# Expert picks by token group inside the feed-forward, bfloat16 slot tables for both choices at once, routing weights made in the routed stage

## The reference, cut to what matters

```python
xn = layernorm(x)                        # eps 1e-5
probs = softmax(xn @ router_w.T)         # 8 experts
val, idx = top_k(probs, 2)               # two experts for each token
w = val / (val.sum(-1) + 1e-8)
for e in range(8):                       # the reference computes all experts
    y[e] = new_gelu(xn @ w1[e].T + b1[e]) @ w2[e].T + b2[e]
out = x + sum over k of w[:, k] * y[idx[:, k]]
```

## Time and profile before

| what | value |
|---|---|
| median of 3 runs | 1114.38 us (1110.06 to 1118.21) |
| the profiled execution | 1115.24 us, span 1113.4 us |
| TensorE busy | 932.3 us (84%) |
| VectorE busy | 569.7 us (51%) |
| ScalarE busy | 574.5 us (52%) |
| GpSimd busy | 620.6 us (56%) |
| second_feed, first and last products near | 585 and 751 us |
| route_second | 751.6 to 781.7 us |
| routed, first transfers to the start of combine | 782.2 to near 1089 us |

### The profile page before, as it was taken

The page is one execution under the profiler, slowest core; times in us unless marked ns, Lnnn a source line. Parts: engine busy times, 40 slices in busy tenths (PEclk is TensorE's granted clock), DMA queues, the critical chain, the costliest instruction groups (busy, mean ns, idle before and its releaser), DMA issues. The chain is left out here.

```text
span 1113.4 us, 20955 instructions
## 1 busy us (share of the span) xinstructions
PE 932.3 (84%) x6700; PEld 843.5 (76%) x6700; DVE 569.7 (51%) x1280; ACT 574.5 (52%) x1201; POOL 620.6 (56%) x605
## 2 busy tenths in 40 slices
PE   6259699998699999969987999941699999999960
PEld 5248467776588988848886999941699999999960
DVE  1335489996555556338764465438233333333325
ACT  0021167776435656547645556630566666666640
POOL 0105658885625554435316998730477778778740
PEclk9669999998779999989997999965799999999985
DMA  7581234443011111100007000043466666666656
GB/s 250 163 296 51 65 134 149 164 147 138 1 58 58 58 58 58 58 1 1 2 1 310 1 15 24 20 180 151 143 189 195 206 194 201 193 191 200 200 154 244
DMA packets 64899, 137.04 MB, mean 123 GB/s; under 512 B 12505, under 2 KB 26578, under 8 KB 63490
## 3 DMA queue, kind: packets, MB, share of 16 engines
q1 hardware_dynamic: 55842, 113.34, 31.6%
q0 software_dynamic: 4848, 14.72, 3.8%
q10 hardware_dynamic: 4144, 8.16, 2.0%
HBM read 114.03 MB, written 24.39 MB: 124 GB/s over the span
## 5 line engine op out<-in xcount | busy, mean ns | idle before, releaser
L122 DVE CAST place<-place 128x512 fp32r<-128x512 f32 (+1 forms) x170 | 89.2, 567 | 166.8 <-PE moe_down L128 101.5
L2337 POOL TENSOR_TENSOR place<-place,place 128x512 fp32r<-128x512 f32 x84 | 138.1, 1644 | 51.5 <-DVE place L122 51.1
L2363 PE MATMUL moe_up<-place,place 128*128 128x128 f32 x1376 | 161.9, 276 | 0.0
L2363 PEld LDWEIGHTS moe_up<-place,place 128*128 128x128 f32 x1376 | 158.3, 193 | 0.0
L128 PE MATMUL moe_down<-place,place 128*128 128x256 f32 x1008 | 131.1, 286 | 0.4 <-POOL place L2337 0.4
L128 PEld LDWEIGHTS moe_down<-place,place 128*128 128x128 f32 x1008 | 123.4, 191 | 0.6 <-issue 0.6
L2422 ACT ACTIVATE place<-place 128x2048 f32 x44 | 84.0, 1912 | 43.6 <-PEq L2159 29.9
L2435 ACT ACTIVATE place<-moe_up,place 128x128 f32<-128x128 f32 x344 | 97.5, 366 | 13.5 <-POOL place L2337 13.2
L1425 POOL TENSOR_TENSOR place<-place,place 128x384 fp32r<-128x384 f32 x42 | 43.4, 1036 | 92.8 <-ACT place L1332 64.1
L787 PE MATMUL scores<-place,place 128*69 128x276 f32 x256 | 68.5, 412 | 11.1 <-DVE place L851 6.7
L1134 PE MATMUL ff_down<-place,place 128*128 128x256 f32 x486 | 70.7, 291 | 5.4 <-POOL place L1425 4.9
(11 more groups left out here) (273 smaller groups left out, 1987.2 us busy)
## 6 DMA issues: line engine op xcount, KB each, us to landing
place<-w_remainder SPq DMA_DIRECT2D x172, 256.0 KB, 3.8
place<-in_w_dram SPq DMA_DIRECT2D x4, 4096.0 KB, 13.3
place<-gate_rows SPq DMA_DIRECT2D x24, 384.0 KB, 4.8
place<-in_w_dram SPq DMA_DIRECT2D x16, 512.0 KB, 3.7
w_remainder<-place SPq DMA_DIRECT2D x16, 512.0 KB, 3.0
place<-value_rows SPq DMA_DIRECT2D x64, 64.0 KB, 2.3
place<-choices ACTq DMA_DIRECT2D x5, 768.0 KB, 8.4
place<-in_patches_dram SPq DMA_DIRECT2D x9, 384.0 KB, 4.1
```

The costliest lines, as they stand in the source:

```text
L122: return eng.tensor_copy(out, x)
L2337: pool.tensor_tensor(lo[f], raw[f], hi[f].bitcast(F32), ALU.subtract).then_inc(h_split, 1)
L2363: last = pe.matmul(p1[u][k // HK][:, (k % HK) * P:(k % HK + 1) * P], ws[u][:, c, k * P:(k + 1) * P], xT[u][:, c, :], start=(c == 0), stop= ...
```

## The change

Three things change.

1. **second_feed** gets a function pick(g) on VectorE: for the three tiles of group g it picks both experts from the logits themselves (the softmax keeps their order), into two one-hot tiles self.hot of bfloat16, and keeps the highest and second highest logit in self.best. It is called for group g - 2 at the end of round g, and for the last two groups at the end. The new tiles lie where head_mask and stats were.
2. **route_second** no longer has the softmax and the choice. hits is the sum of the two one-hot tiles. The small steps of the two choices are made at once on 36 columns. ids, places, blocks and tile numbers are copied to bfloat16, so that the wide comparisons and products read bfloat16 on both inputs. One of the two row tables of each choice is scaled on ScalarE. The owners are computed after the tables.
3. **routed**: the weights (sum of exponentials, reciprocals, products) are made on VectorE ahead of its first split, and TensorE makes rise(0) ahead of turn_x(1).

The diff, cut to its core:

```diff
@@ second_feed, vector
+                def pick(g):
+                    rank = self.rank.unsqueeze(1).to_broadcast([P, G, E])
+                    dve.wait_ge(lg_read, g + 1)
+                    for k, src in enumerate((of(self.lg, g), sc)):
+                        best = self.best[k][:, G * g:G * g + G]
+                        link(dve.tensor_reduce(best, src, AX_X, ALU.max))
+                        link(dve.tensor_tensor(tmp, src, inner(best, E), ALU.is_equal))
+                        link(dve.tensor_tensor(tmp, tmp, rank, ALU.mult))
+                        link(dve.tensor_reduce(top, tmp, AX_X, ALU.max))
+                        link(dve.tensor_tensor(of(self.hot[k], g), inner(top, E), rank, ALU.is_equal))
+                        if k == 0:
+                            link(dve.scalar_tensor_tensor(out=sc, in0=of(self.hot[0], g), scalar=-BIG, in1=src, op0=ALU.mult, op1=ALU.add))
...
                         moments_of(3, x, g + 2)
+                    if g >= 2:
+                        pick(g - 2)
                 add_down(NG - 1)
                 moments_down(NG - 1)
                 add_h(NG - 1)
+                pick(NG - 2)
+                pick(NG - 1)
@@ route_second, scalar
-                act.wait_ge(step, 2)
+                act.activation(spare, self.ident[:, 0:8], ACT.Exp)
+                act.wait_ge(shifted, 2)
                 act.activation(lg, lg, ACT.Exp).then_inc(exped, 1)
+                act.activation(self.best[1], self.best[1], ACT.Exp).then_inc(exped, 1)
+                for k in range(2):
+                    act.wait_ge(matched, k + 1)
+                    act.activation(rows[k][:, :, 0, :], match[:, k], ACT.Copy, scale=consts["row"][:, k:k + 1]).then_inc(scaled, 1)
@@ route_second, vector
-                link(dve.tensor_reduce(total, lg, AX_X, ALU.max))
-                link(dve.tensor_tensor(lg, lg, inner(total, E), ALU.subtract))
+                link(dve.tensor_tensor(hits, self.hot[0], self.hot[1], ALU.add))
                 link(dve.tensor_copy(tri, consts["tri"]))
                 link(dve.memset(ones, 1.0))
...
-                self.choose(lg, first, second, self.weight, tmp, dve, link)
...
+                dve.tensor_tensor(hits[:, NT - 1, :], hits[:, NT - 1, :], consts["valid"][:, NT - 1:NT].to_broadcast([P, E]), ALU.mult).then_inc(hit, 1)
+                dve.tensor_tensor(self.best[1], self.best[1], self.best[0], ALU.subtract).then_inc(shifted, 1)
+                dve.tensor_tensor(lg, lg, inner(self.best[0], E), ALU.subtract).then_inc(shifted, 1)
...
+                for k in range(2):
+                    link.mark(dve.tensor_tensor(spot[:, k], place, self.hot[k], ALU.mult))
+                link.wait()
+                link(dve.tensor_reduce(slot, spot, AX_X, ALU.add))
...
+                for k in range(2):
+                    dve.tensor_tensor(match[:, k], inner(block_id[:, k], XBLK), spread(block_ids, NT), ALU.is_equal).then_inc(matched, 1)
+                dve.wait_ge(ids_ready, 1)
+                dve.tensor_tensor(at_hot[0], inner(at_id[:, 0], P), spread(places, NT), ALU.is_equal).then_inc(hot_ready, 1)
+                for k in range(2):
+                    dve.wait_ge(matched, k + 1)
+                    dve.tensor_tensor(rows[k][:, :, 1, :], match[:, k], inner(tile_ids, XBLK), ALU.mult).then_inc(tiled, 1)
+                dve.tensor_tensor(at_hot[1], inner(at_id[:, 1], P), spread(places, NT), ALU.is_equal).then_inc(hot_ready, 1)
+
                 link(dve.tensor_tensor(past, inner(consts["blocks"], E), spread(fin, XBLK), ALU.is_ge))
                 link(dve.tensor_reduce(own, past, AX_X, ALU.add))
...
@@ routed, tensor
                 turn_x(0, 0, 0)
+                rise(0, 0)
                 turn_x(1, 0, 1)
-                rise(0, 0)
@@ routed, vector
+                link(dve.tensor_reduce(total, self.lg, AX_X, ALU.add))
+                link(dve.reciprocal(self.weight[0], total))
+                link(dve.tensor_tensor(self.weight[1], self.best[1], self.weight[0], ALU.mult))
...
```

## The result

The changed kernel takes 1107.11 us (median of 7 runs, 1105.57 to 1109.87) beside 1114.38 us of the kernel before (7 runs, 1110.06 to 1118.21). The ratio is 0.9941, with a 95% interval of 0.9919 to 0.9963: 4 to 9 us faster, 6.6 by the ratio, and within the 1% called no change. The profiled execution took 1108.34 us with a span of 1106.5, where before it was 1115.24 and 1113.4.

A forecast was written before the change was run, and what follows sets the result against it. VectorE's route chain between two dense TensorE stretches was taken as the bound; 8.4 - 1.5 - 0.6 - 1.1 = 5.2 us gained, and less 0.86 for the runs' median, gave 1109 us, range 1103 to 1114.

The forecast's parts named there:

- What bounds: Between the dense TensorE stretches, one VectorE chain of 30.1 us bounds; each microsecond taken from it shortens the whole time.
- Head: Route's start until hits is written: four instructions instead of 21, 1.0 us instead of 7.33, gain 6.3.
- Picks bare: Last group's pick after the last logits stands bare on the path: route stage starts 2.4 us later.
- Tables: Slot tables in the route: owners moved gain 1.34, joined steps 1.54, scaling on ScalarE 1.10, fewer waits 0.5 us.
- joined small steps: Route's small steps of both choices made at once on 36 columns: 2.76 us instead of 4.30, gain 1.54.
- All terms of the route together: Route: 6.3 - 2.4 + 1.34 + 1.54 + 1.10 + 0.5 = 8.4 us gained.
- Wide tiles, nothing: Route's bfloat16 tiles of 792 and 2304 columns stay at 0.98 and 2.55 us; double-rate rival 4.0 better, chance 0.12.
- Picks in the feed-forward, 1.5: Picks of groups 0 to 2 delay TensorE in the second feed-forward, 0.5 us each, 1.5 lost (0 to 3.6).
- Picks beside the norm, 0.6: Picks of groups 3 and 4 overlap GpSimd's four small norm steps: 0.3 us each, 0.6 lost (0 to 0.9).
- Swap, 1.1: Routed start, first up projection ahead of second turn: 1.1 us lost (bounds 1.1 gained, 1.3 lost).
- Covers: Weights hidden in VectorE's 12 us wait at the routed start, owners in a 1.59 us wait with 0.25 left.
- The signs: Prediction wrong if picks hide wholly, wide tiles halve, or TensorE's routed dense stretch starts no later after the route.

The follow-up runs named there:

- e7_picks_in_route: Changed kernel without the swap and with no pick in the feed-forward; all 18 tiles' picks run at the start of route_second: 1105.6 us.
- e5_tile_inner: Changed kernel with the 18 tiles as inner dimension of match, rows and at_hot, so no input repeats an element there: 1106.56 us.
- e3_before_swap: Kernel before the change with only the swap, rise(0) ahead of turn_x(1): 1116.97 us, 1.0021 against the kernel before.
- e1_no_swap: Changed kernel with the old order, turn_x(1) ahead of rise(0) again at the start of the routed stage: 1104.53 us.

## Why the prediction was right

- **What bounds.** The chain from the last logits to the end of the route was the place to look: 8.6 of the gain is there.
- **Head.** Hits was said 1.0 after the stage's start and is written 0.95 after it, and the counts are read 1.98 after that, as before.
- **Picks bare.** 2.4 taken. The pick takes 2.34 and the stage starts 3.00 after the last logits, as said.
- **Tables.** The stage from first to last instruction was said to take 19.2 and takes 19.09. The joined small steps, said 2.76, take 2.68 (758.81 to 761.49); the other terms of the tables no run takes apart. All terms of the route together: 8.4 said, 8.57 measured. `e7_picks_in_route` splits it: without groups 7.2 of it are left (30.66 - 23.50); the groups bring the other 1.4, and their picks in the feed-forward take 0.9 back.
- **Wide tiles, nothing.** Measured 0.94 and 2.55. `e5_tile_inner` shows the reason given to be the right one: the same types without a repeated inner element ran at 0.53 and 1.35. Both pages of the Trainium skill named in the prediction are borne out, each in its own case: the tier table of "VectorE: DVE Perf Modes" by `e5_tile_inner`, section 5.1 of "Vector Engine (DVE) Microarchitecture Reference" by the changed kernel.
- **Picks in the feed-forward, 1.5.** The mechanism is as told: one instruction of a pick held by GpSimd's subtraction (0.92 and 1.04), the pick 3.1 to 3.2 us long, TensorE late by the overrun. That is 0.42 in each of two rounds; the third pick is 2.6 long, one instruction takes 0.46, and it ends 0.89 before it is waited for. 0.85, not 1.5.
- **Picks beside the norm, 0.6.** Nothing: GpSimd's four small steps of the last norm take 1.84 (741.89 to 743.73), before 1.81. From the fifth read of the down projection to the last logits it is 38.50 us and was 38.45.
- **Swap, 1.1.** The mis-sized term. The step that failed is "its two parts would end near 794.1, not 795.4": it moved products measured at one time to an earlier time and kept their duration, 4.95. They took 5.71 in the changed kernel and 6.69 in `e3_before_swap`, because more of them ran before the clock rose (in `e3_before_swap` it also rose 2 us later). So most of the early end doesn't exist, and the turn, the copy and the table load behind it come that much later: 2.7 us by the table load's place and 2.9 at the last read, and 2.6 by the medians. The place of the table load, said to be 12.7 to 13.5 after the route (13.3 by its sum), was missed with it: 14.7. Of the 1.5 that are missing, 0.8 is the longer products (5.71 for 4.95) and 0.6 a first turn that came later after the route (6.86, before 6.22), which the swap can't have caused, since nothing that it moves comes before that turn.
- **Covers.** The weights lie on VectorE at 778.28 to 780.25, ten microseconds ahead of the first cast that it makes for the experts; the owners fit in their wait with 0.46 left. Both held.

- **The signs.** Of what the prediction called proof against it, neither hidden picks nor halved tiles came. Its third, a dense stretch of TensorE that starts no later after the route, is met for one reading and not for the other: the first products start 8.09 us after the route's end (before 8.75), the first down projection 19.76 (before 17.25). The time follows the second: the last read comes 2.9 later.

Two terms erred in opposite directions, picks and roots by 1.2 too dear, the swap by 1.8 too cheap (of which 0.6 is the late first turn), and that they nearly cancel is luck. The steps gave 5.2 where the three stretches show 4.8; the median is another 2 lower for reasons outside the change. So the route's part was right by its mechanism, and the total is better than its terms.

## What to carry to other kernels

Before an order of products is given a gain, look at the granted clock where they would run, not where they ran: here 0.5 us was left of 1.3. When one instruction is moved on one engine, the other engines' in-order queues must be moved with it: the swap needed ScalarE's copy to move too. A layout is to be costed on both of its readers; here turning the tables helped VectorE twofold for either table, and only the one that TensorE reads as weights kept the gain. And one trace of each of two kernels doesn't price an edit below a microsecond: the same feed-forward took 124.49 to 125.94 us here.

## What the runs showed of the hardware

- A bfloat16 moving operand of 88 columns, read with a stride of 18 elements (36 bytes), makes a product 165 to 168 ns long (waits within the 36 included) instead of 82 to 84, all at a granted clock of 0.50; the same stride in the 128 x 128 weights shows no difference.
- VectorE's tensor-tensor comparison in bfloat16: 1.35 us for 2304 columns with the repetition of one input in an outer dimension, 2.55 when one input repeats its element along the inner one.
- A two-input instruction of VectorE and one of GpSimd that become ready 0.01 us apart run one after the other, and which goes first differs between executions of the same instructions (changed kernel: addition 0.96 beside a subtraction of 1.84; `e1_no_swap`: 1.82 beside 1.02). That is a swing of 0.85 us on the path here, as large as what the picks cost.
- The granted clock stood at 0.50 through the route and the wait for the gather, and went to 1.00 between 5.1 and 7.2 us after the first turn in the traces of all twelve kernels, with the up projection started early or late.
